# Attention edge stage stores its packed sums as columns, and the output product moves to the node stage

## The chip, the cores and the metric

One core of a Trainium2 chip runs the whole network as one program. The metric is the device time of one execution in microseconds (us), the median of several runs. Besides, one execution was recorded by the hardware profiler; all rows shown here are from that one.

## The reference

Four graph layers follow each other over 50000 nodes and 50000 edges, which are sorted by destination. All numbers are 32-bit floats and D is 128. The change touches the second layer, whose attention is:

```python
K = (x @ Wk.T + bk).reshape(N, HEADS, HEAD_DIM)
V = (x @ Wv.T + bv).reshape(N, HEADS, HEAD_DIM)
Q = x.reshape(N, HEADS, HEAD_DIM)
scores = jnp.sum(K[src] * Q[dst], axis=-1) / np.sqrt(HEAD_DIM)
m = jax.ops.segment_max(scores, dst, num_segments=N)
e = jnp.exp(scores - m[dst])
denom = jax.ops.segment_sum(e, dst, num_segments=N)
attn = e / (denom[dst] + 1e-16)
out = jax.ops.segment_sum(V[src] * attn[:, :, None], dst, num_segments=N)
return out.reshape(N, DIM_H) @ Wo.T + bo
...
h = _batchnorm(x + h_attn, bn1_g, bn1_b)
```

The other layers and the feed-forward part are not touched.

## The kernel before

The program is a row of stages, each with its own block: one in-order instruction stream per engine, semaphores between the streams, and a barrier at the end. A step handles 512 rows (TILES = 4 tiles of P = 128), and S = 98 steps cover all. Two stages matter.

**The attention edge stage** (`attention_edges`, tiles named `e_`) is written as a software pipeline of STEPS = S + 36 loop turns n. In turn n each engine does the pieces of several steps, in the order of the source. TensorE (PE) does: `e_s`, the scores of step n-4 (L1459); `e_hs`, transposes of the gathered source rows of step n (L1467); `e_k` of n-2 (L1474); `e_hd`, transposes of the destination rows of n (L1480); `e_r`, the output product with `wo` of n-33 (L1488); `e_v` of n-29 (L1496); and `e_p`, the packing of n-31 (L1506). Packing sums the weighted messages of a run of equal destinations: a matmul with the 0/1 matrix `pick`, whose column c is 1 where an edge belongs to the c-th run. A step is packed in two halves of HALF = 256 columns; the last column of each holds the sum of the run that goes on in the next half. So many edges can't have more runs than edges, so the first 128 edges of a half fill none of the columns 128 to 254. VectorE (DVE) does in turn n: `e_kq` (L1302), the scan `e_hdt` (L1310), `e_pv` (L1320, messages times weights), `carry_step` of n-32 (L1288, L1290: the open run is added to column 0 in PSUM), then a piece of the softmax of a whole group of GROUP = 14 steps in 11 of every 14 turns, and last `pick` (L1343, L1346). ScalarE (ACT) copies PSUM tiles out (`e_hst`, `e_packed` from `e_r`, `e_att` from `e_p` with the bias `bv`) and issues four loads or stores a turn. GpSimd (POOL) issues four gathers a step (L659), at most four steps ahead of `e_hs`. SyncE (SP) stores each packed half at the row where its first run begins. The halves overlap, so each store waits until the one before it has landed (semaphore `placed`):

```python
for h in range(HALVES):
    if w or h:
        sp.wait_ge(placed, (w * HALVES + h) * 16)
    sp.dma_start(run_rows(scratch["att_runs"], begins[h], HALVES),
                 at(packed, w)[:, HALVES * h:HALVES * h + HALVES, :]).then_inc(placed, 16)
```

Gathers and `e_hs`, `e_k`, `e_hd` end with turn 97; `e_v` begins with turn 29 and `e_p` with turn 31. Turns 31 to 97 are called the full turns below, those from 98 on the closing turns. ps_p, the PSUM tile of `e_p`, is one bank, so `e_p` of a step waits for `e_att` of the step before.

**The attention node stage** (`attention_nodes`, tiles named `n_`): for each 512 nodes SP loads two tiles of runs and the old features `n_h`, ACT loads the other two tiles of runs (its own queue), PE transposes `n_h` and spreads the runs to their nodes with a second 0/1 matrix (`n_t`, L1646), ACT adds the bias `bo` (`n_own`), DVE adds both (`n_tt`, L1619) and ACT stores it. ACT's stream in loop turn i is: load the start rows from SBUF into registers, issue the loads of runs of step i, then `n_own` of step i-3, then the store of step i-5. There are four buffers of runs.

Of the kernel before, what the change touches and what calls it, by code (L numbers as in the profile page):

```python
# [16 lines left out]
P = 128  # L17
# [1027 lines left out]
def attention_edges(nc, size, a, scratch, k):  # L1045
# [10 lines left out]
    with Phase(nc, "e1") as ph:  # L1056
# [13 lines left out]
        att, att_ready = ph.made("att", [D, ROWS])  # L1070
        packed, packed_ready = ph.made("packed", [P, TILES, D], 6)
# [4 lines left out]
        v_done, pack_done, out_done, carry_done = (ph.sem(n) for n in ("v_done", "pack_done", "out_done", "carry_done"))  # L1076
# [31 lines left out]
        ps_hs, ps_hd, ps_k, ps_v, ps_p, ps_r = (ph.ps(n) for n in ("hs", "hd", "k", "v", "p", "r"))  # L1108
# [18 lines left out]
        STEPS = S + 36  # L1127

        @block.sync
        def _(sp):  # L1130
# [23 lines left out]
        def _(dve):  # L1154
# [122 lines left out]
            def carry_step(j):  # L1277

                g, t = divmod(j, GROUP)
                dve.wait_ge(pack_done, j + 1)  # L1280
                if t == 0 and g:
# [3 lines left out]
                for h in range(HALVES):  # L1285
                    own = flat(ps_p)[:, h * HALF:(h + 1) * HALF]
                    new = carry[(j * HALVES + h) % 3]
                    dve.scalar_tensor_tensor(new[:, :], held[0][:, :], half[:, j, HALVES + h:HALVES + h + 1],  # L1288
                                             own[:, HALF - 1:HALF], ALU.mult, ALU.add)
                    done(dve.scalar_tensor_tensor(own[:, 0:1], held[0][:, :], half[:, j, h:h + 1], own[:, 0:1],  # L1290
                                                  ALU.mult, ALU.add))
                    held[0] = new
                dve.sem_inc(carry_done, 1)

            for n in range(STEPS):
# [44 lines left out]
                if 0 <= j < S:  # L1340
                    dve.wait_ge(at(row_in, j), moved(j, j))
                    for t in range(TILES):
                        dve.tensor_scalar(at(pick, j)[:, t, 0:HALF - 1], k.place_row[:, 0:HALF - 1],  # L1343
                                          at(row, j)[:, RUN_SLOT * TILES + t:RUN_SLOT * TILES + t + 1].bitcast(F32), None,
                                          ALU.is_equal)
                    dve.tensor_copy(at(pick, j)[:, :, HALF - 1], values(at(row, j), TAIL)).then_inc(pick_ready, 1)  # L1346

        @block.scalar
        def _(act):
# [12 lines left out]
            for n in range(STEPS):  # L1362
# [66 lines left out]
        def _(pe):  # L1429
# [22 lines left out]
            for n in range(STEPS):  # L1452
# [46 lines left out]
                if 0 <= j < S:  # L1499
                    pe.wait_ge(pv_ready, j + 1)  # L1500
                    pe.wait_ge(pick_ready, j + 1)
                    if j:
                        pe.wait_ge(att_ready, j)
                    for t in range(TILES):
                        h = t // HALVES
                        ins = pe.matmul(flat(ps_p)[:, h * HALF:(h + 1) * HALF], at(pv, j)[:, t, :], at(pick, j)[:, t, :],  # L1506
                                        start=(t % HALVES == 0), stop=(t % HALVES == HALVES - 1))
# [1207 lines left out]
```

## Time and profile before

| | us |
|---|---|
| median of 3 runs (lowest, highest) | 6114.3 (6105.96, 6123.12) |
| the profiled execution: its own time | 6110.7 |
| its span, first to last instruction | 6108.8 |
| edge stage of the attention, first gather to the last store's issue | 1470.2 to 2293.0 |
| node stage of the attention, first issue to last | 2297.3 to 2564.5 |

A stage's time is not visible in the shares of the whole page, since ten other stages are mixed in. The two stages together take about 1100 us of the span and have to be read by windows and by the timeline. "busy" of matmuls is modelled and overlaps, so PE's true pitch is read from the distance of starts. A matmul of 32-bit floats appears as two instructions (x8 for four of them); transposes as one.

### The profile page before, as it was taken

To read this page: it belongs to the slowest core of one execution; us is meant where nothing else is said; L and a number is where in the kernel's file an instruction comes from. 1 tells how busy PE (TensorE), PEld (TensorE's weight loads), DVE (VectorE), ACT (ScalarE), POOL (GpSimd) and SP (SyncE) were. 2 spreads that over 40 slices of the span, in tenths; PEclk is the share of its full clock that TensorE was granted. 3 is DMA by queue.
4 is the path that set the end of the run, shared out by engine and by line. 5 is a ranking of instruction groups with operands and counts; after the bars stand their busy time and mean duration, and the time that the engine had idled before them with its cause. 6 is when DMAs were issued, how large, how long until landed. Compare 5 with 4: busy or idle time off the path is not lost. (4 is left out here: it accounts for less than half of the span.)

```text
span 6108.8 us, 80252 instructions
## 1 busy us (share of the span) xinstructions
PE 3926.9 (64%) x16966; PEld 2588.9 (42%) x16966; DVE 3885.2 (64%) x12531; ACT 1981.9 (32%) x4351; POOL 3027.9 (50%) x2764
## 2 busy tenths in 40 slices
PE   2777733332699985599544457888564877777840
PEld 1555522221377774444333356766321333333310
DVE  4666657773488866667444456666596766766656
ACT  1545422331122222255444432222264222222210
POOL 3566436666666500000455558888402566666630
PEclk7888955555799999999766779899897888888875
DMA  8666656664566528877555557777695011111149
GB/s 268 131 140 140 133 148 191 184 182 143 149 173 176 162 58 266 270 229 226 188 181 171 172 155 130 132 132 131 166 373 196 22 30 33 35 36 37 38 146 375
DMA packets 930549, 954.27 MB, mean 156 GB/s; under 512 B 166711, under 2 KB 617031, under 8 KB 930111
## 3 DMA queue, kind: packets, MB, share of 16 engines
q1 hardware_dynamic: 539178, 545.18, 31.1%
q10 hardware_dynamic: 259157, 259.51, 12.6%
q0 software_dynamic: 131904, 146.31, 12.1%
q8 instruction: 89, 1.46, 0.1%
q14 instruction: 221, 1.81, 0.1%
HBM read 544.69 MB, written 440.07 MB: 161 GB/s over the span
## 5 line engine op out<-in xcount | busy, mean ns | idle before, releaser
L667 POOL DMA_INDIRECT at_first_table<-n_h,n_first_edge x784 | 803.0, 1024 | 1413.2 <-ACT n_h L277 832.0
L2559 PE MATMUL e_m<-e_by_rel,rel_w 128*128 128x512 f32 x1568 | 756.1, 639 | 0.7 <-issue 0.5
L2473 DVE SCALAR_TENSOR_TENSOR e_by_rel<-e_y,e_part_t 128x512 f32<-128x512 f32 x784 | 477.5, 680 | 310.3 <-DMA sum_table<-n_own 223.9
L659 POOL DMA_INDIRECT e_xs<-x_table,e_idx x392 | 381.1, 972 | 434.4 <-DMA e_idx<-idx_table 299.1
L667 POOL DMA_INDIRECT rel_sum_table<-e_res,scat_placed x392 | 393.9, 1005 | 315.4 <-ACT e_res L2525 197.9
L659 POOL DMA_INDIRECT e_x<-x,e_idx x392 | 405.5, 1034 | 279.3 <-issue 172.0
L659 POOL DMA_INDIRECT e_hs<-h_table,e_idx x392 | 420.0, 1071 | 228.6 <-issue 120.1
L947 PE MATMUL n_m<-n_mean,n_pick 128*128 128x129 f32 x784 | 204.7, 442 | 446.7 <-DVE n_pick L1012 231.8
L2559 PEld LDWEIGHTS e_m<-e_by_rel,rel_w 128*128 128x128 f32 x1568 | 318.6, 209 | 371.2 <-issue 371.1
L277 ACT ACTIVATE n_h<-n_x,n_norm_shift,n_norm_rstd 128x128 f32<-128x128 f32 x784 | 322.7, 482 | 182.7 <-issue 116.4
L947 PEld LDWEIGHTS n_m<-n_mean,n_pick 128*128 128x128 f32 x784 | 175.6, 329 | 475.8 <-DVE n_pick L1012 246.9
L2048 PE MATMUL n_o<-w_center_cat,n_h2t 128*128 128x128 f32 x784 | 165.8, 377 | 318.9 <-ACT n_h2t L2015 266.9
L253 ACT ACTIVATE e_norm_std<-e_norm_moments,eps 128x4 f32<-128x4 f32 x196 | 58.3, 297 | 962.3 <-DVE e_norm_moments L245 509.1
L675 POOL DMA_INDIRECT sum_table<-e_res,e_target x196 | 305.0, 1556 | 94.0 <-issue 59.8
L675 POOL DMA_INDIRECT sum_high_table<-e_res,e_target x196 | 312.3, 1593 | 61.8 <-issue 55.1
L2048 PEld LDWEIGHTS n_o<-w_center_cat,n_h2t 128*128 128x128 f32 x784 | 142.2, 272 | 346.9 <-ACT n_h2t L2015 214.4
L2551 PE MATMUL e_t<-ident,e_part 128*128 128x128 f32 x392 | 79.5, 339 | 215.6 <-ACT e_part_t L2513 111.3
L238 DVE BATCH_NORM_STATS2 e_norm_stats<-e_x 128x6 f32<-128x128 f32 x392 | 85.3, 280 | 202.1 <-DMA e_x<-x,e_idx 182.0
L253 ACT ACTIVATE n_norm_std<-n_norm_moments,eps 128x4 f32<-128x4 f32 x294 | 86.0, 292 | 377.6 <-DVE n_norm_moments L245 257.8
L2303 PE MATMUL e_s<-e_same,e_msg 128*128 128x256 f32 x784 | 205.1, 409 | 0.0
L869 PE MATMUL e_c<-e_res,e_pick 128*128 128x130 f32 x392 | 94.9, 330 | 166.6 <-issue 96.1
L2270 PE MATMUL e_p<-w_node,e_hdt 128*128 128x128 f32 x784 | 116.5, 294 | 132.7 <-DVE e_hdt L2206 132.7
(390 smaller groups left out, 10118.1 us busy)
## 6 DMA issues: line engine op xcount, KB each, us to landing
x_table<-n_x ACTq DMA_DIRECT2D x294, 256.0 KB
n_x<-x_table SPq DMA_DIRECT2D x294, 256.0 KB
mean_runs_table<-e_packed SPq DMA_DIRECT2D x196, 130.0 KB
n_mean<-mean_runs_table SPq DMA_DIRECT2D x392, 65.0 KB
at_first_table<-zero ACTq DMA_DIRECT2D x1, 25088.0 KB
e_edge<-edge128T SPq DMA_DIRECT2D x98, 256.0 KB
e_keep<-col_tab_table SPq DMA_DIRECT2D x196, 128.0 KB
n_x<-x SPq DMA_DIRECT2D x98, 256.0 KB
```

What stands on the lines that cost most here:

```text
L253: act.activation(at(self.std, u)[:, :], at(self.moments, u)[:, :, 1], ACT.Sqrt, bias=k.eps[:, :]).then_inc(self.std_done, 1)
L277: last = act.activation(out[:, t, :], x[:, t, :], func, bias=at(self.shift, u)[:, t:t + 1], scale=at(self.rstd, u)[:, t:t + 1])
L659: pool.indirect_dma_start(out=tile[:, t, :], out_offset=None, in_=table, in_offset=bass.IndirectOffsetOnAxis(ap=idx[:, col + t:col + t + 1 ...
L667: pool.indirect_dma_start(out=table, out_offset=bass.IndirectOffsetOnAxis(ap=idx[:, t:t + 1], axis=0), in_=tile[:, t, :], in_offset=None, ...
L675: pool.indirect_dma_start(out=table, out_offset=bass.IndirectOffsetOnAxis(ap=idx[:, t:t + 1], axis=0), in_=tile[:, t, :], in_offset=None, ...
L869: pe.matmul(ps_c[b][:, 0, :], at(pick, u - 10)[:, b, 0:P], at(res, u - 10)[:, low, :], start=True, stop=False)
L947: ins = pe.matmul(at(ps_m, u - 1)[t // HALVES][:, t % HALVES, :], at(pick, u - 1)[:, t, :], at(mean, u - 1)[:, t, 0:D + 1], start=True, st ...
L2048: ins = pe.matmul(at(ps_o, u - 3)[:, t, :], at(h2t, u - 3)[:, t, :], k.w_center_cat[:, :], start=True, stop=True)
L2270: ins = pe.matmul(ps_p[:, t, :], at(hdt, u - 1)[:, t, :], k.w_node[:, :], start=True, stop=True)
L2303: ins = pe.matmul(flat(at(ps_s, u))[:, half], at(msg, u)[:, t, :], at(same, u - 2)[:, t, :], start=(t % 2 == 0), stop=(t % 2 == 1))
L2473: ins = dve.scalar_tensor_tensor(at(by_rel, u - 5)[:, r, :], flat(ps_y), float(r), at(part_t, u - 5)[:, :], ALU.is_equal, ALU.mult)
L2559: ins = pe.matmul(flat(at(ps_m, u - 6)), k.rel_w[:, r, :], at(by_rel, u - 6)[:, r, :], start=(r == 0), stop=(r == RELS - 1))
```

## The change

In the edge stage `e_r` and `e_att` go. The packing matmul per half becomes three: 129 columns of the first 128 edges, the same 129 of the other 128 edges added to them, and the last 127 columns of the other 128 edges alone. The open-run column moves from 255 to 0, and the other columns by one. `ps_p` becomes two banks in turn. ACT copies 2 x 255 columns with the bias `bv` to `packed` ([D, 2, 255]), two turns earlier than before, and STEPS is S + 33. SP stores [128 partitions x 255 floats], 1020 bytes a partition, into a table that is now [D, runs], so a half is 128 pieces of 1020 bytes, 202752 bytes apart, beginning at any multiple of 4 bytes; before it was 256 rows of 512 bytes in one stretch. DVE builds `pick` 128 wide for two of the four tiles and 255 wide for the other two. In `carry_step` the wait for the last operation moves to the start of the next step's.

In the node stage a tile of runs is [D, 128 columns], loaded as 128 pieces of 512 bytes from the same table. PE multiplies it with `wo` (`n_w`), ACT copies that to `n_rows`, and PE spreads it two turns later. Buffers of runs come free at `wo_done`. ACT does `n_own` and `n_rows` of step i-1 where it did `n_own` of step i-3.

```diff
@@ attention_edges, SP @@
-                    sp.dma_start(run_rows(scratch["att_runs"], begins[h], HALVES),
-                                 at(packed, w)[:, HALVES * h:HALVES * h + HALVES, :]).then_inc(placed, 16)
+                    sp.dma_start(scratch["att_runs"][:, bass.ds(begins[h], HALF - 1)], at(packed, w)[:, h, :]
+                                 ).then_inc(placed, 16)
@@ carry_step, DVE @@
                 dve.wait_ge(pack_done, j + 1)
+                if j:
+                    dve.wait_ge(carry_done, j)
...
-                dve.sem_inc(carry_done, 1)
+                    if h < HALVES - 1:
+                        done(ins)
+                ins.then_inc(carry_done, 1)
@@ pick, DVE @@
                     for t in range(TILES):
-                        dve.tensor_scalar(at(pick, j)[:, t, 0:HALF - 1], k.place_row[:, 0:HALF - 1],
+                        there = P if t % HALVES == 0 else HALF - 1
+                        dve.tensor_scalar(at(pick, j)[:, t, 1:1 + there], k.place_row[:, 0:there],
@@ ACT @@
-                j = n - 34
-                if 0 <= j < S:
-                    act.wait_ge(out_done, j + 1)
-                    if j >= 6:
-                        act.wait_ge(placed, (j - 5) * HALVES * 16)
-                    act.activation(at(packed, j)[:, :, :], ps_r[:, :, :], ACT.Copy).then_inc(packed_ready, 1)
                 j = n - 32
                 if 0 <= j < S:
                     act.wait_ge(carry_done, j + 1)
-                    if j >= 2:
-                        act.wait_ge(out_done, j - 1)
-                    act.activation(at(att, j)[:, :], flat(ps_p), ACT.Identity, bias=k.bv[:, :]).then_inc(att_ready, 1)
+                    if j >= 6:
+                        act.wait_ge(placed, (j - 5) * HALVES * 16)
+                    act.activation(at(packed, j)[:, :, :], at(ps_p, j)[:, :, 1:HALF], ACT.Identity, bias=k.bv[:, :]
+                                   ).then_inc(packed_ready, 1)
@@ PE @@
-                j = n - 33
-                if 0 <= j < S:
-                    pe.wait_ge(att_ready, j + 1)
-                    if j:
-                        pe.wait_ge(packed_ready, j)
-                    for t in range(TILES):
-                        ins = pe.matmul(ps_r[:, t, :], at(att, j)[:, t * P:(t + 1) * P], k.wo[:, :], start=True, stop=True)
-                    ins.then_inc(out_done, 1)
...
-                    if j:
-                        pe.wait_ge(att_ready, j)
+                    if j >= 2:
+                        pe.wait_ge(packed_ready, j - 1)
@@ attention_nodes, PE @@
+                    if begun(i - 3):
+                        pe.wait_ge(rows_ready, i - 2)
                     for t in range(TILES):
+                        ins = pe.matmul(at(ps_w, u)[:, t, :], at(runs, u)[:, t, :], k.wo[:, :], start=True, stop=True)
+                    ins.then_inc(wo_done, 1)
+                j = i - 2
+                if live(j, S):
+                    pe.wait_ge(pick_ready, j + 1)
+                    pe.wait_ge(rows_ready, j + 1)
@@ attention_nodes, ACT @@
                     if begun(i - 4):
-                        act.wait_ge(spread_done, i - 3)
+                        act.wait_ge(wo_done, i - 3)
...
-                j = i - 3
+                j = i - 1
                 if live(j, S):
                     act.wait_ge(turned, j + 1)
...
+                    act.wait_ge(wo_done, j + 1)
+                    if begun(j - 3):
+                        act.wait_ge(spread_done, j - 2)
+                    act.activation(at(rows, u - 1)[:, :, :], at(ps_w, u - 1)[:, :, :], ACT.Copy).then_inc(rows_ready, 1)
```

PE's stream of one full turn of the edge stage, before:

```order
L1459 MATMUL e_s<-e_kq,e_head_win 112x512
L1467 MATMUL e_hs<-ident,e_hs 128x128 x4
L1474 MATMUL e_k<-e_hst,wk 128x512
L1480 MATMUL e_hd<-ident,e_hd 128x128 x4
L1488 MATMUL e_r<-wo,e_att 128x128 x4
L1496 MATMUL e_v<-wv,e_hst 128x128 x4
L1506 MATMUL e_p<-e_pick,e_pv 128x256 x4
```

And of the changed kernel, the same turn:

```order
L1459 MATMUL e_s<-e_kq,e_head_win 112x512
L1467 MATMUL e_hs<-ident,e_hs 128x128 x4
L1474 MATMUL e_k<-e_hst,wk 128x512
L1480 MATMUL e_hd<-ident,e_hd 128x128 x4
L1488 MATMUL e_v<-wv,e_hst 128x128 x4
L1498 MATMUL e_p<-e_pick,e_pv 128x129
L1499 MATMUL e_p<-e_pick,e_pv 128x129
L1501 MATMUL e_p<-e_pick,e_pv 128x127
L1498 MATMUL e_p<-e_pick,e_pv 128x129
L1499 MATMUL e_p<-e_pick,e_pv 128x129
L1501 MATMUL e_p<-e_pick,e_pv 128x127
```

`e_r` is gone and the 1024 packing columns have become 770.

ACT's stream of one turn of the node stage, before (from the register loads to the store):

```order
L165 TENSOR_LOAD starts
L165 ISA x4
L1659 ISA
L1659 DMA n_runs<-att_runs_table 128x128
L1659 ISA
L1659 DMA n_runs<-att_runs_table 128x128
L1666 ACTIVATE n_own<-n_h,bo 128x512
L1671 DMA tt_table<-n_tt 128x512
```

And of the changed kernel:

```order
L165 TENSOR_LOAD starts
L165 ISA x4
L1664 REGISTER_ALU
L1664 DMA n_runs<-att_runs_table 128x128
L1664 REGISTER_ALU
L1664 DMA n_runs<-att_runs_table 128x128
L1671 ACTIVATE n_own<-n_h,bo 128x512
L1676 ACTIVATE n_rows<-n_w 128x512
L1680 DMA tt_table<-n_tt 128x512
```

One instruction more, and the two ACTIVATEs belong to the step whose runs were issued one turn before, where the one of before belonged to the step of three turns before.

## Rows read from the trace of the kernel before

**Rows 1.** Windows: length, busy PE, PEld, DVE, ACT, POOL, then PEclk, DMA share, GB/s.

```profile
1700.00:2090.00 390.00, 377.80 (x2210) 284.28 (x2209) 334.96 (x867) 110.65 (x192) 259.01 (x230) 1.00 0.63 177
2130.00:2295.00 165.00, 136.69 (x812) 114.19 (x810) 105.97 (x365) 41.61 (x71) 0.00 (x0) 0.96 0.21 56
2310.00:2570.00 260.00, 151.35 (x1136) 134.10 (x1135) 176.38 (x282) 64.78 (x95) 0.00 (x0) 0.97 0.91 285
```

**Rows 2.** Timeline of PE, one full turn: start, length, line, operation, count.

```profile
1905.35 1.11 PE L1459 MATMUL e_s<-e_kq,e_head_win 128*112 128x512 f32 x2
1908.03 1.06 PE L1488 MATMUL e_r<-wo,e_att 128*128 128x128 f32 x8
1908.92 1.06 PE L1496 MATMUL e_v<-wv,e_hst 128*128 128x128 f32 x8
1909.82 1.89 PE L1506 MATMUL e_p<-e_pick,e_pv 128*128 128x256 f32 x8
1911.64 0.20 PE L1444 MATMUL e_x<-ident,e_top 112*1 112x8 f32 x2
```

**Rows 3.** Timeline of DVE in the same turn.

```profile
1909.84 1.13 DVE L1343 TENSOR_SCALAR e_pick<-place_row,e_row 128x255 f32<-128x255 f32 x4
1910.89 0.16 DVE L1346 COPY e_pick<-e_row 128x4 f32<-128x4 f32 x1
```

**Rows 4.** Groups by line, 1700 to 2090 us: count, busy, mean ns, idle before.

```profile
L659 POOL DMA_INDIRECT e_hs<-h_table,e_idx x230 | 261.6, 1137 | 131.3 <-issue 73.1 <-PE e_hs L1467 58.2
L1320 DVE TENSOR_TENSOR e_pv<-e_v,e_weight_t 128x512 f32<-128x512 f32 x57 | 38.5, 675 | 40.0 <-remote 35.1 <-PE e_p L1506 2.7 <-issue 2.2
L1264 DVE RECIPROCAL e_spare<-e_back 112x512 f32<-112x512 f32 x4 | 13.4, 3352 | 0.1
```

**Rows 5.** Waits of SP's queue, 1700 to 2090 us: total, times, longest.

```profile
SPq L1140 <- DMA att_runs_table<-e_packed: 52.6, 26, 3.7
SPq L1139 <- DMA att_runs_table<-e_packed: 28.8, 19, 3.1
```

**Rows 6.** Timeline of ACT and PE, closing turns.

```profile
2232.53 0.69 ACT L1397 ACTIVATE e_att<-e_p,bv 128x512 f32<-128x512 f32 x1 [3.18 <-DVEq L1293]
2233.36 1.96 PE L1506 MATMUL e_p<-e_pick,e_pv 128*128 128x256 f32 x8 [0.28 <-ACT e_att L1397]
2236.89 0.69 ACT L1397 ACTIVATE e_att<-e_p,bv 128x512 f32<-128x512 f32 x1 [3.18 <-DVEq L1293]
```

**Rows 7.** SP's stores at the end of the edge stage, and in all; the last ACT copies.

```profile
2270.69 22.67 SPq L1140 DMA_DIRECT2D att_runs_table<-e_packed  x12
...
L1140 SPq DMA_DIRECT2D att_runs_table<-e_packed x196: 3/372/701, 1695.0 to 2293.0; - x196
L1368 ACT ACTIVATE e_hst<-e_hs x98: 597/597/600, 1477.9 to 2126.8; 128x512 f32<-128x512 f32 x98
```

**Rows 8.** Node stage: SP's issues of runs, duration and first and last start.

```profile
L1595 SPq DMA_DIRECT2D n_runs<-att_runs_table x196: 332/333/2312, 2297.3 to 2564.5; - x196
```

**Rows 9.** Timeline at the start of the node stage, SP and PE.

```profile
2298.28 0.43 SPq L1599 DMA_DIRECT2D n_h<-h_table  x1
2301.24 1.11 PE L1638 MATMUL n_h<-ident,n_h 128*128 128x128 f32 x4 [15.39 <-DMA n_h<-h_table]
```

**Rows 10.** Timeline of ACT and PE inside the node stage.

```profile
2423.10 1.06 PE L1646 MATMUL n_t<-n_pick,n_runs 128*128 128x128 f32 x8
2423.30 0.69 ACT L1666 ACTIVATE n_own<-n_h,bo 128x512 f32<-128x512 f32 x1 [2.16 <-PE n_h L1638]
2423.31 0.36 ACTq L1671 DMA_DIRECT2D tt_table<-n_tt  x1
2424.82 0.86 ACTq L1659 DMA_DIRECT2D n_runs<-att_runs_table  x2
```

**Rows 11.** SP's queue by window: earlier node stage (820 to 1420 us), then this one (2310 to 2570).

```profile
q1 hardware_dynamic: 67802, 49.80, 33.8%
q1 hardware_dynamic: 40301, 36.81, 47.7%
```

More of the change, by code:

```diff
@@ L1107, in attention_edges @@
              "den_back_col", "weight_turned", "factor_spread"))
-        ps_hs, ps_hd, ps_k, ps_v, ps_p, ps_r = (ph.ps(n) for n in ("hs", "hd", "k", "v", "p", "r"))
+        ps_hs, ps_hd, ps_k, ps_v = (ph.ps(n) for n in ("hs", "hd", "k", "v"))
+        ps_p = [ph.ps(f"p{u}", (D, HALVES, HALF)) for u in range(2)]
         ps_s, ps_x = ph.ps("s", (P, ROWS)), ph.ps("x", (P, ROWS))
@@ L1285, in carry_step @@
                 for h in range(HALVES):
-                    own = flat(ps_p)[:, h * HALF:(h + 1) * HALF]
+                    own = at(ps_p, j)[:, h, :]
                     new = carry[(j * HALVES + h) % 3]
                     dve.scalar_tensor_tensor(new[:, :], held[0][:, :], half[:, j, HALVES + h:HALVES + h + 1],
-                                             own[:, HALF - 1:HALF], ALU.mult, ALU.add)
-                    done(dve.scalar_tensor_tensor(own[:, 0:1], held[0][:, :], half[:, j, h:h + 1], own[:, 0:1],
-                                                  ALU.mult, ALU.add))
+                                             own[:, 0:1], ALU.mult, ALU.add)
+                    ins = dve.scalar_tensor_tensor(own[:, 1:2], held[0][:, :], half[:, j, h:h + 1], own[:, 1:2],
+                                                   ALU.mult, ALU.add)
                     held[0] = new
-                dve.sem_inc(carry_done, 1)
+                    if h < HALVES - 1:
+                        done(ins)
+                ins.then_inc(carry_done, 1)
             for n in range(STEPS):
@@ L1342, in _ @@
                     for t in range(TILES):
[L1343 removed]
+                        there = P if t % HALVES == 0 else HALF - 1
+                        dve.tensor_scalar(at(pick, j)[:, t, 1:1 + there], k.place_row[:, 0:there],
                                           at(row, j)[:, RUN_SLOT * TILES + t:RUN_SLOT * TILES + t + 1].bitcast(F32), None,
                                           ALU.is_equal)
[L1346 removed]
+                    dve.tensor_copy(at(pick, j)[:, :, 0], values(at(row, j), TAIL)).then_inc(pick_ready, 1)
         @block.scalar
@@ L1501, in _ @@
                     pe.wait_ge(pick_ready, j + 1)
-                    if j:
-                        pe.wait_ge(att_ready, j)
[L1504 to L1507, printed above, removed]
+                    if j >= 2:
+                        pe.wait_ge(packed_ready, j - 1)
+                    for h in range(HALVES):
+                        low, high, own = HALVES * h, HALVES * h + 1, at(ps_p, j)[:, h, :]
+                        pe.matmul(own[:, 0:P + 1], at(pv, j)[:, low, :], at(pick, j)[:, low, 0:P + 1], start=True, stop=False)
+                        pe.matmul(own[:, 0:P + 1], at(pv, j)[:, high, :], at(pick, j)[:, high, 0:P + 1], start=False,
+                                  stop=True)
+                        ins = pe.matmul(own[:, P + 1:HALF], at(pv, j)[:, high, :], at(pick, j)[:, high, P + 1:HALF],
+                                        start=True, stop=True)
                     ins.then_inc(pack_done, 1)
@@ L1576, in attention_nodes @@
         h1, h1_in = ph.loaded("h1", [P, TILES, D])
-        runs, low_in = ph.loaded("runs", [P, TILES, D])
+        runs, low_in = ph.loaded("runs", [D, TILES, P])
         high_in = ph.dma_sems("high_in")
         pick, pick_ready = ph.made("pick", [P, TILES, P], 4)
-        own, own_ready = ph.made("own", [D, TILES, P])
+        own, own_ready = ph.made("own", [D, TILES, P], 4)
+        rows, rows_ready = ph.made("rows", [P, TILES, D], 3)
         tt, tt_ready = ph.made("tt", [D, TILES, P], 4)
         tt_out = ph.dma_sems("tt_out")
-        turned, spread_done, stats_done = ph.sem("turned"), ph.sem("spread_done"), ph.sem("stats_done")
-        ps_h, ps_t = ph.banks("h"), ph.banks("t")
+        turned, wo_done, spread_done, stats_done = (ph.sem(n) for n in ("turned", "wo_done", "spread_done", "stats_done"))
+        ps_h = ph.banks("h")
+        ps_w, ps_t = ([ph.ps(f"{n}{u}") for u in range(3)] for n in ("w", "t"))
         block = ph.ctx.enter_context(nc.Block())
@@ L1592, in body @@
                     if begun(i - 4):
-                        sp.wait_ge(spread_done, i - 3)
+                        sp.wait_ge(wo_done, i - 3)
                     for t in range(HALVES):
-                        sp.dma_start(at(runs, u)[:, t, :], scratch["att_runs"][bass.ds(begins[t], P), :]
+                        sp.dma_start(at(runs, u)[:, t, :], scratch["att_runs"][:, bass.ds(begins[t], P)]
                                      ).then_inc(at(low_in, u), 16)
@@ L1641, in body @@
                     pe.wait_ge(at(high_in, u), moved(i, u, HALVES))
-                    pe.wait_ge(pick_ready, i + 1)
-                    if begun(i - 2):
-                        pe.wait_ge(tt_ready, i - 1)
+                    if begun(i - 3):
+                        pe.wait_ge(rows_ready, i - 2)
                     for t in range(TILES):
-                        ins = pe.matmul(at(ps_t, u)[:, t, :], at(runs, u)[:, t, :], at(pick, u)[:, t, :], start=True,
-                                        stop=True)
+                        ins = pe.matmul(at(ps_w, u)[:, t, :], at(runs, u)[:, t, :], k.wo[:, :], start=True, stop=True)
[5 more added lines that the diff above has]
+                    if begun(j - 3):
+                        pe.wait_ge(tt_ready, j - 2)
+                    for t in range(TILES):
+                        ins = pe.matmul(at(ps_t, u - 2)[:, t, :], at(rows, u - 2)[:, t, :], at(pick, u - 2)[:, t, :],
+                                        start=True, stop=True)
                     ins.then_inc(spread_done, 1)
-            each_step(body, S, 0)
+            each_step(body, S, 2)
         @block.scalar
```

18 lines of the change are left out of this document (9 added, 9 removed).

## The prediction

> **What bounds the kernel now.** The change lives in two stages, so I read windows first. In the full turns of the edge stage PE is busy 378 of 390 us at full clock, DVE 335, POOL 259, and the DMA engines are busy 63% of the time; in the node stage it is the other way round, DMA 91% and PE 151 of 260 us [rows 1]. The reader is to see that the edge stage is short of engine time and the node stage of transfers, and that the change moves work from the first to the second.
>
> Next the timeline of one full turn. PE starts `e_s` at 1905.35 and has finished `e_p` at 1911.64, 6.29 us without a gap [rows 2]. 57 `e_pv` in 390 us are 6.84 us a turn [rows 1, 4], so a turn is somewhat longer than PE's own work. The rest is DVE: in 11 of 14 turns it has a piece of the group's softmax to do, and one of these holds a reciprocal of 3.35 us and several scans [rows 4]; such turns are DVE's. DVE's only wait of size is the 40.0 us before `e_pv` [rows 4], which comes after the previous turn's `e_p`, the last thing that PE does in a turn. So the full turns alternate: a turn costs what the slower of PE and DVE needs in it, and DVE's idle time (0.70 us a turn, 40.0 over 57) is what a faster PE can give at most.
>
> In the closing turns the pitch of `e_att` is 4.36 us [rows 6] and PE and DVE go round in a ring: `e_p` waits for `e_att`, `e_att` for `carry_step`, that for `e_p`. But right beside it is SP: twelve stores in 22.67 us, the last issue taking 0.37, make 2.03 us from store to store, 4.06 a turn [rows 7]. The last store is issued at 2293.0, the last `e_hst` at 2126.8 [rows 7]: 166 us of closing.
>
> In the node stage SP issues 196 loads of runs in 267.2 us, 2.76 us a step [rows 8]. ACT there waits 2.16 us for `n_h` before it does `n_own` [rows 10], and that costs nothing, because it works three steps behind its own loads.
>
> **Full turns.** Removed from PE: eight instructions of `e_r`, 1908.03 to 1908.92, 0.89 us. `e_p` takes 1.82 us for eight instructions, of which the last part is the change to `e_x`; 1024 columns become 770, and twice as many columns per instruction as in `e_v` took twice as long, so I take 1.82 x 770/1024 = 1.37, a saving of 0.45 [rows 2]. PE's turn falls from 6.29 to 4.95. If six weight loads per step instead of four were to limit it, the saving on `e_p` would be nothing; that is the other bound, and still leaves 5.4, under DVE's mean.
>
> DVE: four `pick` pieces take 1.05 us, 0.26 each [rows 3]. Two become half as wide: 0 to 0.26 saved, I take 0.15 as part of a short instruction is fixed. The last handshake of `carry_step` goes off its path, about 0.1. ACT loses one copy and is busy 28% of the window [rows 1]: nothing. DVE's mean turn without waits was 6.84 - 0.70 = 6.14; less 0.25 it is 5.9. In the three turns of 14 without softmax, and in a few with a short piece, DVE needs about 4.15 and PE 4.95, so roughly 0.2 a turn of waiting remains: 6.1. I add 0.05 for the other two chains, which come near. POOL is busy 261.6 us and stands 73.1 us between instructions for nothing that is shown, 5.9 us a turn [rows 4]; it waits 58.2 us for `e_hs`, which is the slack it has. SP waits 81.4 us for stores to land in this window [rows 5], so under the load of the other transfers a store takes more than the 2.03 us of the end. So 6.15 instead of 6.84: 0.69 x 67 turns (31 to 97) = **-46 us**. Bounds: 5.9 gives -63, 6.45 (POOL or SP as the bound) gives -26.
>
> **Closing turns.** The ring opens: `e_p` has two banks, `e_att` and `e_r` are gone. PE's work falls to `e_v` and `e_p`, 0.89 + 1.37, DVE's to about 2.3 outside the softmax pieces. What comes next is SP with its serial stores. Each is 128 pieces of 1020 bytes in place of 256 of 512; no row shows such a piece, and I bound it by the row of now, 2.03 us, plus or minus 0.2. From the last `e_hst` on 31 to 32 steps are to be stored, 4.06 to 4.2 each, about 130, and the turn with the reciprocal, once at the start, holds SP up by some 9: 139 instead of 166, **-27 us**. Bounds: -38 with quicker stores, -14 with slower.
>
> **Node stage.** SP's and the other queues' bytes are the same. PE gets `n_w`, priced as `n_t`, 8 instructions of 0.11 at full clock, 0.89 us: 2.2 us of PE in a step of 2.76, covered. ACT gets a copy of 0.59 us. The price is in the order. Before, ACT had three steps between its loads of runs and the first wait that stands behind them. Now, in turn i, it issues runs i and then waits for `wo_done` of step i-1, whose runs it issued one turn before; runs i+1 stay queued behind that wait. So two turns can't be shorter than one trip round: from the first to the second issue 0.45, landing L, `n_w` 0.9 and a semaphore 0.1, the issue of `tt` and after it the register loads until the next runs, which were 1.51 us from 2423.31 to 2424.82 [rows 10]; in sum 3.0 + L. What is L? At the stage's start, with little in flight, `n_h` was issued at 2298.28 and used by PE at 2301.24: 2.96 us [rows 9]. Inside the stage the queue on the engines is longer, DMA share 0.91 [rows 1]. A store of 128 KB landed and was followed up in 2.03 [rows 7], the low end. I take L = 3.5, since a longer step lowers the load but the run loads now stand behind `tt` in the same queue: (3.0 + 3.5)/2 = 3.25 us a step, +0.49 x 98 = **+48 us**. Bounds: L of 2.5 gives 2.75, no cost at all; L of 4.5 gives 3.75, +97.
>
> **Against the rules.** The Trainium skill, "DMA: Bandwidth & Descriptors", section Anatomy of one DMA, gives a fixed cost of about 2.0 us and a variable one of bytes over 436 GB/s. By it a 64 KB load lands after 2.15 us (an estimate of that page), the round trip would be (3.0 + 2.15)/2 = 2.6, below 2.76, and the stage would not lengthen. The row says 2.96 for 256 KB at light load, 0.4 more than the page's 2.6 for that size, and so L of the loaded stage lies above it too.
>
 In the earlier node stage SP's queue loads rows of 520 bytes, which begin anywhere: 33.8% of 16 engines over 600 us for 49.80 MB are 65 us per MB, against 47.7% over 260 us for 36.81 MB, 54 us per MB, with aligned rows [rows 11]. The sizes are mixed differently, so the rows allow such a cost and don't prove it.
>
> **Rivals.**
> 1. The node stage hides its new wait (runs land within 2.5 to 2.9 us when the load eases). For it: the 2.96 of [rows 9] is of a transfer four times as large. Against: DMA share 0.91. Then +0 to +19, net about -60: 6055. Chance 0.2.
> 2. Node stage decides, slower than before: the wait on `wo_done` with L at 4.3 or more. That is the point where (3.0 + L)/2 = 3.65, +87, outweighs what a somewhat weaker edge stage gives (-65). For it: ACT already waits 2.2 us for a transpose that itself waits for a load [rows 10]; and if pieces at odd places take half as long again, the runs' third of the bytes lengthens the queue. At L = 4.8 the stage costs +112 and the net is +39: 6153. Chance 0.18.
> 3. The full turns don't follow PE. POOL's 5.9 and SP's serial stores under load become the bound at 6.5. For it: [rows 4, 5]. Against: both have slack of four and six steps. Then -23 - 27 + 48 = about 0: 6113. Chance 0.17.
> 4. The forecast, -46 - 27 + 48 = -25. Chance 0.45.
>
> **Numbers.** The profiled execution took 6110.7; less 25 is 6086. It stands 3.6 below the median of the runs, so 6089 in terms of that. The forecast's own range is 6065 to 6112. With the rivals' share on both sides, 6045 to 6145. A difference under 0.3%, 18 us, can't be told from no change. The forecast lies for the larger part beyond it (0.28 of 0.45), rival 1 wholly, rival 3 hardly (0.03), rival 2 never: faster 0.51. Same: 0.17 of the forecast, 0.13 of rival 3, 0.02 of rival 2: 0.32. Slower: 0.17.
>
> **What the changed profile would show.** Full turns: start-to-start of PE's `e_s` at 6.1 on average, PE's work in it 5 us, the wait before `e_pv` down from 40 us to under 15 in 57 turns, DVE busy over 90%. Closing turns: SP's stores one after the other at 2.0 us with ACT's `e_packed` waiting for them. Node stage: SP's 196 loads of runs over about 315 us in place of 267, ACT's queue waiting for `n_w` before `n_rows`, PE waiting for ACT's runs and no longer for `n_h`, and a DMA share near 0.78. The prediction is wrong if the node stage keeps its 2.76 us a step, if stores of 1020-byte pieces take clearly other than 2.03 us, or if the full turns stay above 6.4.

## The result, and the profile after

The changed kernel took 6145.6 us (median of 6 runs, 6137.22 to 6158.71), the kernel before 6115.11 beside it: ratio 1.0054, interval 1.0041 to 1.0068, so slower by half a per cent. The forecast was 6089, in a range of 6045 to 6145. In a second set of runs the ratio was 1.0078 (1.0050 to 1.0107). In a third set, on a chip that had run the kernel before in 6103 us earlier, the kernel before took 5629.73 us and the ratio was 0.9994 (0.9984 to 1.0005). One and the same program runs at two levels, 9% apart, and the change is worth something else at each; this turned out to be the core of the case. I call these the slower and the faster level; all runs that were made together, one after the other on one chip, lay at the same one.

Where the time went in the profiled executions at the slower level, before and after in us:

| | before | after | difference | forecast |
|---|---|---|---|---|
| start of the edge stage to its 33rd `e_hst` | 1477.9 to 1686.8 | 1473.9 to 1681.0 | -2 | 0 |
| full turns, 33rd to 98th `e_hst` | 440.0 | 441.6 | +2 | -46 |
| closing, last `e_hst` to the last store | 166.2 | 146.3 | -20 | -27 |
| node stage, first runs to the last store of `tt` | 274.1 | 332.8 | +59 | +48 |

The rest, -4 ahead of the stage and +6 behind it, lies in stages that the change doesn't touch.

The windows of the changed kernel, as in [rows 1], and the groups by line of DVE and POOL, 1700 to 2090 us, as in [rows 4]:

```profile
1700.00:2090.00 390.00, 323.68 (x1946) 236.71 (x1947) 317.15 (x849) 81.10 (x132) 238.06 (x226) 0.96 0.61 174
2126.00:2272.00 146.00, 90.00 (x665) 80.42 (x664) 98.36 (x364) 24.76 (x38) 0.00 (x0) 0.90 0.20 62
2285.00:2590.00 305.00, 229.85 (x1826) 214.39 (x1826) 170.62 (x272) 111.99 (x182) 0.00 (x0) 0.97 0.81 236
```

```profile
L1314 DVE TENSOR_TENSOR_SCAN e_hdt<-e_keep,e_hdt,e_hd 128x512 f32<-128x512 bf16 x56 | 71.0, 1267 | 12.9 <-remote 12.9
L1324 DVE TENSOR_TENSOR e_pv<-e_v,e_weight_t 128x512 f32<-128x512 f32 x57 | 38.6, 676 | 47.9 <-remote 39.1 <-PE e_p L1501 6.2 <-issue 2.5
```

```profile
L659 POOL DMA_INDIRECT e_hs<-h_table,e_idx x226 | 238.9, 1057 | 152.1 <-PE e_hs L1467 60.0 <-issue 60.0 <-remote 32.2
```

The reader is to see that PE did lose the work (378 of 390 us busy before, 324 now) and that no engine took its place: PE 83%, DVE 81%, POOL 61%, transfers 61%. DVE waits more than before, 47.9 us before `e_pv` and 12.9 before `e_hdt` where it had 40.0 and nothing, and 52 us of that have a "remote" releaser. A piece of the timeline shows what stands behind this word (DVE, POOL and PE; start, length, line):

```profile
1702.75 0.39 PE L1501 MATMUL e_p<-e_pick,e_pv 128*128 128x127 f32 x2
1704.30 0.60 PE L1467 MATMUL e_hs<-ident,e_hs 128*128 128x128 f32 x4
1705.45 0.94 POOL L659 DMA_INDIRECT e_hs<-h_table,e_idx  x1 [0.30 <-issue]
1705.59 0.60 PE L1480 MATMUL e_hd<-ident,e_hd 128*128 128x128 f32 x4
1707.79 0.69 DVE L1324 TENSOR_TENSOR e_pv<-e_v,e_weight_t 128x512 f32<-128x512 f32 x1 [2.96 <-remote]
1708.58 0.94 POOL L659 DMA_INDIRECT e_hs<-h_table,e_idx  x1 [2.18 <-remote]
1708.63 1.13 PE L1488 MATMUL e_v<-wv,e_hst 128*128 128x128 f32 x8 [2.43 <-DVE e_pv L1324]
```

PE's `e_p` is recorded as ended at 1703.14, but the trace's record of its semaphore stands at 1707.66, and those of `e_s`, `e_hs`, `e_k` and `e_hd` behind it at 1707.75 to 1707.91, all at once. (The profile writes "remote" where the semaphore that ended a wait has no instruction that ended shortly before.) DVE waits for the first of them, POOL for `e_hs`, PE then for DVE: from 1706.40 to 1707.79 none of the three works. I call this a late release. To count them over the turns from the 34th to the 98th `e_hst`, each of PE's products is matched with the first record of its semaphore behind its recorded end and ahead of the next turn's; records are missing, so not all can be matched. 119 of 355 came over 1 us late in the changed kernel, 43 of 386 in the kernel before.

### The profile page after: what moved, and what is told of

Same layout as the page of the kernel before. It is cut to its first block and busy times, and to the rows that moved or that the text cites. A ratio compares the mean times of both kernels' runs of the same rounds, so it can differ in the third digit from the quotient of the medians.

```text
span 6149.7 us, 80931 instructions
## 1 busy us (share of the span) xinstructions
PE 3900.5 (63%) x17358; PEld 2589.7 (42%) x17358; DVE 3866.4 (63%) x12531; ACT 1986.0 (32%) x4351; POOL 3014.4 (49%) x2764
## 5 line engine op out<-in xcount | busy, mean ns | idle before, releaser
L667 POOL DMA_INDIRECT at_first_table<-n_h,n_first_edge x784 | 802.7, 1024 | 1457.7 <-ACT n_h L277 870.5
L659 POOL DMA_INDIRECT e_hs<-h_table,e_idx x392 | 402.2, 1026 | 246.6 <-issue 104.1
L2568 PEld LDWEIGHTS e_m<-e_by_rel,rel_w 128*128 128x128 f32 x1568 | 317.9, 209 | 370.0 <-issue 370.0
```

The source lines that it names most:

```text
L659: pool.indirect_dma_start(out=tile[:, t, :], out_offset=None, in_=table, in_offset=bass.IndirectOffsetOnAxis(ap=idx[:, col + t:col + t + 1 ...
L667: pool.indirect_dma_start(out=table, out_offset=bass.IndirectOffsetOnAxis(ap=idx[:, t:t + 1], axis=0), in_=tile[:, t, :], in_offset=None, ...
L2568: ins = pe.matmul(flat(at(ps_m, u - 6)), k.rel_w[:, r, :], at(by_rel, u - 6)[:, r, :], start=(r == 0), stop=(r == RELS - 1))
```

## The experiments

The measure for the full turns is the distance from the 33rd to the 98th `e_hst`, divided by 65. All edits are made to the changed kernel, if nothing else is said.

| us a full turn | slower level | faster level |
|---|---|---|
| kernel before | 6.77, 6.85 | 6.60 |
| changed kernel | 6.79, 6.74 | 5.98 |
| with the node stage's longer lag | 6.75, 6.86 | 5.93 |
| and a later start of the gathers (behind `e_v`; behind `e_p`) | 6.97; - | 5.92; 5.92 |
| `e_v` done twice | 7.00 | - |
| zero stores moved out | 6.73 | - |
| one gather of four | - | 6.03, 6.05 |
| no gathers | 6.00 | - |
| kernel before, no gathers | - | 6.63, 6.64, 6.63 |

**Is PE what sets the full turn?** (e_v2)

```diff
-                    for t in range(TILES):
+                    for t in range(2 * TILES):
+                        t = t % TILES
                         ins = pe.matmul(ps_v[:, t, :], at(hst, j)[:, t * P:(t + 1) * P], k.wv[:, :], start=True, stop=True)
```

> The changed kernel, with the four products e_v of each turn of the edge stage done twice (1.06 us more of PE's work a turn, the same result). If PE's work sets the full turn, as the forecast had it, 6.79 us a turn becomes 7.6 to 7.9 us. If PE has slack that the change opened (1.34 us less work a turn for no gain), it stays within 6.75 to 7.0 us. The closing turns (4.0 us bound by SP's stores, PE at 60%) should stay at 146 us by both.

Measured: 7.00 us a turn, at the top of the second range; 1.06 us more work cost 0.21. PE has the slack: most of the added work is hidden. The whole took 6160.69 us in one run; closing was 153 us, 7 more than expected.

**Gathers out** (e_plain; the same for the kernel before in e_before_plain, q_before_plain and z_before_plain)

```diff
-                gather(pool, at(hs, i), scratch["h1"], idx[:, i, :], 0, at(hs_in, i))
...
                 act.dma_start(at(hd, i)[:, :, :], in_order(scratch["at_first"], i)).then_inc(at(hd_in, i), 16)
+                act.dma_start(at(hs, i)[:, :, :], in_order(scratch["h1"], i)).then_inc(at(hs_in, i), 16)
```

> The changed kernel; in the edge stage the source rows are not gathered by POOL's four indirect transfers a turn but loaded by one plain transfer of 512 rows in order, issued by ACT behind e_hd's (so other rows are attended: the gather is left out, the bytes stay). Full turns are counted on e_hst from its 33rd to its 98th instruction: 6.79 us in the changed kernel, 6.77 before. Theory POOL: PE's finished products are handed over late while POOL issues its gathers (the releases come about 1.1 us behind the fourth gather's end), and these holds make DVE's waits of 49 us in the 380 us looked at; without gathers the turn falls to 6.2 us or less. Theory transfers: the 16 DMA engines' load or the landings set the turn; the bytes are the same, so it stays at 6.7 or more. Theory DVE: DVE's own work with its start-up gaps is 6.1 a turn and ACT's order the rest; 6.6 to 6.8.

Measured: 6.00 us, 5993.63 in all. DVE's waits in the full turns, total, times, longest, and the window itself:

```profile
DVE e_pv L1323 <- PE e_p L1501: 12.4, 16, 0.8
DVE e_kq L1305 <- PE e_k L1474: 7.8, 11, 1.9
```

```profile
1600.00:1960.00 360.00, 328.72 (x2055) 243.50 (x2054) 333.00 (x897) 86.25 (x141) 0.00 (x0) 0.97 0.65 199
```

No remote releaser is left, and with the same bytes, or nearly, the transfers' share is even a little higher. DVE is busy 92%, as forecast for the changed kernel. Counted as above, none of 437 semaphores of PE came over 1 us late. So the turn that the forecast wanted (6.15) exists, and the gathers stand between it and the kernel at this level. What the edit takes out is both POOL's issuing and the scattered transfers themselves.

> The kernel before, with the same replacement as in the changed kernel without gathers: the edge stage's source rows come by one plain transfer of 512 rows in order, issued by ACT (the gather is left out, other rows are attended). If the gathers' holds hid the change's gain, the full turns of this kernel stay above the 6.00 us of the changed one, since here PE has its 6.29 us of work a turn: 6.4 to 6.6 us, and the change is then worth 0.4 to 0.6 us a turn where POOL issues nothing. If PE's work never mattered, both stand at 6.0 to 6.1 us.

This run fell on the faster level (the kernel before took 5607.38 us beside it): 6.63 us, 5538.38 in all. Two more runs, meant for the slower level, fell on the faster one too: 6.64 and 6.63.

> The kernel before without gathers in the edge stage (a plain transfer in their place), once more: the first run of it fell on a chip that runs the kernel before in 5607 us. On a chip of 6110 us, where the changed kernel without gathers had full turns of 6.00 us: theory POOL expects 6.5 to 6.7 us here (PE's pace, no holds), so that the change is worth 0.5 to 0.7 us a turn once nothing is gathered, as the forecast had it. If the chip and not the gathers set both, 6.0 to 6.1.

> The kernel before without the edge stage's gathers, for the one cell that is missing. Where the kernel before takes 6110 us: if the late releases come only with POOL's gathers, its full turns stand at 6.6 us, as they do (twice, 6.63) where the kernel before takes 5620 us, against 6.00 us of the changed kernel without gathers; 6.75 to 6.85 us if something else holds them. Where it takes 5620 us: 6.63 a third time.

So the kernel before stands at 6.63 us where nothing is gathered, with PE as its pace, and the cell at the slower level stays empty.

**Less load from transfers** (e_nozero)

```diff
-                if n < S:
-                    act.dma_start(rows_of(scratch["rel_sum"], n), k.zero[:, :]).then_inc(zeroed, 16)
+            for n in range(S):
+                act.dma_start(rows_of(scratch["rel_sum"], n), k.zero[:, :]).then_inc(zeroed, 16)
```

> The changed kernel, with the 98 stores of zeros to rel_sum taken out of the edge stage's turns and issued by ACT in a row behind its loop (same bytes, other place). That takes one of ACT's four transfer issues, 0.46 us, and 256 KB out of each turn. Theory transfers: the full turn falls by 0.3 us or more from 6.79. Theory POOL (holds while the gathers are issued): it stays within 0.1 us. Theory ACT's order (e_hst waits behind e_packed and the issues): it falls by some 0.2 us. The end of the stage becomes longer by the stores' own time, 50 to 90 us, so the total tells nothing.

Measured: 6.73 us, within 0.1 of 6.79, with the window's DMA share at 0.51 in place of 0.61 (1700 to 2080 us), and DVE still waits 47 us there for remote releasers. Neither this load nor ACT's order explains the missing 0.6 us a turn. (6166.25 us in all.)

**The node stage's order** (e_node; again as r_node and z_node). The first piece is PE's `n_t`, the second ACT's `n_own` and `n_rows`; their buffer indices go along.

```diff
                     ins.then_inc(wo_done, 1)
-                j = i - 2
+                j = i - 3
...
-                j = i - 1
+                j = i - 2
                 if live(j, S):
                     act.wait_ge(turned, j + 1)
```

> The changed kernel, with one more turn between the output product and its reader in the node stage: ACT's n_own and n_rows go from step i-1 to step i-2, PE's spread product n_tt from i-2 to i-3. Nothing else. In-order theory: the wait on wo_done of the step just loaded stands before the next loads, and that costs 3.28 us a step against 2.76 in the kernel before; with two steps in hand the loads of n_runs go back to 2.8 us a step or less, the stage gives back 45 to 55 us, and the kernel takes 6092 to 6102 us, 0.2 to 0.4% under the kernel before. Rival, column loads themselves are slow (512 B pieces of 128 partitions, a third product and copy): the pitch stays at 3.1 us or more and the kernel stays over 6125 us.

Measured: 6113.71 us, ratio 1.0012 (0.9988 to 1.0037). SP's issues of runs, to be read beside [rows 8]; first the changed kernel, then this one:

```profile
L1592 SPq DMA_DIRECT2D n_runs<-att_runs_table x196: 332/333/1592, 2273.1 to 2591.0; - x196
```

```profile
L1592 SPq DMA_DIRECT2D n_runs<-att_runs_table x196: 332/333/1165, 2273.2 to 2554.3; - x196
```

Over 97 steps that is 3.28 against 2.90 us. The longer lag gives back 34 us from the first runs to the last store of `tt` (332.8 to 298.8; 27 us of the whole in a later set that had both kernels, 6157.8 and 6130.77), less than the 45 to 55 expected, and the whole stayed over the 6092 to 6102; 0.15 us a step above the kernel before stay. The order is shown as the larger part of the price, not as all of it.

**Does it matter when the gathers start?** (e_late_v and r_late_v, on top of the longer lag; e_late_pack waits for `pack_done` at i - 34 instead)

```diff
                     pool.wait_ge(hs_turned, i - 3)
+                if i >= 33:
+                    pool.wait_ge(v_done, i - 32)
```

> The changed kernel with the node stage's longer lag, and in the edge stage POOL starts the gathers of turn i+4 only when PE has ended e_p of turn i's step (before: when e_hs was turned, half a turn earlier). All four gathers stay. Theory POOL: the holds then fall on e_s, e_hs, e_k, e_hd of the next turn, which DVE wants some 4 us later, and no longer on e_p and e_v: 6.3 to 6.6 us a full turn against 6.79 (6.75 in the kernel with the longer lag). If the start makes no difference, since POOL's four gathers fill 4.7 of the turn wherever they begin: 6.7 to 6.9 us.

> As the one above, but POOL starts when PE has ended e_v (about 1.4 us earlier in PE's turn). The hold then falls on e_p, whose carry DVE does some 2.8 us later: 6.4 to 6.7 us a full turn if the place counts, and more than with the start behind e_p; 6.7 to 6.9 us if it doesn't.

Measured: 5.92 us both, 5568.15 and 5565.76 in all. It looked like a success, but beside them the kernel before took 5607.38 us, not 6110, and not one semaphore of PE's was late (none of 431 and 436). The next set was to separate the two:

> The kernel before, unchanged, for its trace beside the others of this call on the same chip: one chip ran it in 6103 us (median of 13), another in 5607 us. Where the chip is one that runs it in about 5600 us, theory holds expects: no wait of DVE's e_pv put down to a remote releaser (35 us in the 380 us looked at, in the first trace), early turns of 5.2 us instead of 6.5 (as in the two late-start kernels), and full turns that still stand at 6.6 to 6.8 us, PE's own pace (6.63 in this kernel without gathers). Where it is one of about 6110 us: 6.77 as in the first trace.

> The changed kernel, unchanged. On a chip of 5600 us theory holds expects what the forecast had: full turns of 5.9 to 6.1 us (PE and DVE free to follow, -0.6 to -0.7 a turn, some -45 us), closing turns -20 us, node stage +50 to +55 us, in sum -10 to -20 us against the kernel before. If the holds aren't what separates the chips, the full turns stand within 0.1 us of the kernel before and the changed kernel is 30 us slower there too. On a chip of 6110 us: +0.5%, as measured.

> The changed kernel with the longer lag in the node stage (n_own, n_rows at i-2, spread at i-3). Node stage 2.9 to 3.0 us a step against 3.2 to 3.3, so 20 to 35 us less than the changed kernel on any chip; against the kernel before -35 to -50 us on a chip of 5600 us, within 0.3% on one of 6110 us.

> The kernel with the longer lag and POOL's gathers started only when PE has ended e_v, beside the same without the later start on the same chip. It ran at 5.92 us a full turn on the chip of 5600 us. If the later start did that, the kernel above stands at 6.3 us or more there; if the chip did it, the kernel above stands within 0.1 us of this. On a chip of 6110 us the start counts only if the full turn falls from 6.75 to under 6.6 us.

It fell on the slower level. Kernel before 6.85 us a full turn (6107.4 in all); changed kernel 6.74, ratio 1.0078; longer lag 6.86, ratio 1.0029 (1.0013 to 1.0045), node stage 2.91 us a step; later start 6.97, ratio 1.0036 (1.0015 to 1.0057). The later start gives nothing (0.11 us a turn more, no more than the two traces of the kernel with the longer lag differ from each other); the 5.92 was the level's. My idea that the place of the gathers in PE's turn counts is refuted for the start behind `e_v`; the start behind `e_p` was not run at this level.

**Both kernels at the faster level** (q_before, q_after, q_g1)

> The kernel before, unchanged, for its trace on this call's chip. Full turns of 6.6 to 6.85 us on any chip: PE's own pace lies at 6.6, the holds add little since PE is behind them all the same. Early turns, which wait for landings, 5.2 us on a chip of 5600 us and 6.4 on one of 6110.

> The changed kernel, unchanged. On a chip of 5600 us: full turns of 5.9 to 6.1 us, so that the change gains 40 to 50 us there, against 50 lost in the node stage and 20 gained behind the last turn: 0.2 to 0.4% faster than before. On a chip of 6110 us: full turns of 6.7 to 6.85 us and 0.5 to 0.8% slower, as twice measured.

Measured: 6.60 and 5.98 us a full turn, ratio 0.9994 (0.9984 to 1.0005). DVE's waits in the full turns, first the kernel before, 1600 to 1960 us, then the changed one, 1600 to 1930, and the windows of the latter (full turns, node stage):

```profile
DVE e_pv L1320 <- PE e_p L1506: 25.8, 23, 1.9
DVE e_pv L1320 <- issue: 0.9, 1, 0.9
```

```profile
DVE e_pv L1324 <- PE e_p L1501: 11.7, 16, 0.8
DVE e_kq L1306 <- PE e_k L1474: 6.2, 10, 1.6
```

```profile
1600.00:1930.00 330.00, 301.73 (x1887) 224.74 (x1887) 305.90 (x824) 79.30 (x129) 229.57 (x218) 0.96 0.72 197
2110.00:2390.00 280.00, 211.95 (x1683) 197.01 (x1682) 158.16 (x252) 103.39 (x169) 0.00 (x0) 0.97 0.82 239
```

No remote releaser in either, with all four gathers on POOL; late semaphores 0 of 494 and 0 of 434. DVE is busy 93%. The differences by part: full turns -40, closing -23 (169.7 to 147.0), node stage +56 (273.4 to 329.8), in sum -6 of 5630, while the median moved by -2. So here the forecast's step for the full turns holds, and the node stage eats it; the gain of 0.2 to 0.4% that I expected did not come.

DVE's work in a full turn is the same at both levels: 5.5 us, from its busy share in the windows above and 6.79 and 5.98 us a turn. Its idle time is 1.27 us at the slower and 0.44 at the faster, and this is the whole of the 0.81 between the two.

> The changed kernel with one gather of four left on POOL. On a chip of 6110 us (none: 6.00, four: 6.74 to 6.79): theory POOL expects 6.0 to 6.2 us a full turn and under 5 us of waits of DVE with a remote releaser in 380 us (27 to 39 us with four gathers). A turn above 6.4 us would say that one gather costs as much as four.

6.05 us, the same as with the first run of it:

> The changed kernel, with one of the four gathers of a turn kept on POOL and the other three tiles loaded by one plain transfer of ACT's (three quarters of the gather are left out; the bytes stay). Theory POOL: a hold lasts from the product to about 1.1 us behind POOL's last gather, so with one gather of 0.94 us in place of four in 4.7 us the holds have under 2.1 us to cover, most of it hidden: 6.0 to 6.2 us a full turn (four gathers 6.79, none 6.00). If it were the gathers' transfers, and not POOL's issuing, a quarter of them would leave a quarter of the 0.79 us, the same 6.2; a turn over 6.4 us would speak against both, for a price of the first gather.

6.03. Both ran at the faster level, where four gathers cost no more (5.98), so they say nothing on how the late releases depend on the number of gathers.

**The version that keeps both gains** (z_node)

> The changed kernel with the longer lag in the node stage, once more, against the kernel before on this call's chip. Where the kernel before takes about 5620 us: full turns of 5.98 us as in the changed kernel there (6.60 in the kernel before), node stage 2.9 to 3.0 us a step (3.25 without the lag, 2.75 before), so 40 us from the full turns and 20 from the closing ones stand against 20 in the node stage: 5575 to 5600 us, 0.5 to 0.8% faster than before. Where it takes about 6110 us: the full turns give nothing, and it stands at +0.0 to +0.4%, as twice measured.

5567.6 us against 5596.85, ratio 0.9932 (0.9911 to 0.9954), inside the expected gain and 7 us under the expected time, since the kernel before was faster here too. Full turns 5.93 us, node stage 2.97 us a step:

```profile
L1592 SPq DMA_DIRECT2D n_runs<-att_runs_table x196: 332/333/1141, 2050.2 to 2338.6; - x196
```

```profile
2080.00:2330.00 250.00, 203.18 (x1644) 190.68 (x1642) 154.02 (x247) 95.98 (x162) 0.00 (x0) 0.97 0.88 260
```

The transfers' share is back at 0.88, near the 0.91 of [rows 1]. This kernel beats both others at the faster level; at the slower it stands at +0.1 and +0.3%.

## Why the prediction was wrong

**Full turns: the step that failed.** "DVE's idle time (0.70 us a turn, 40.0 over 57) is what a faster PE can give at most", and then that PE's fall from 6.29 to 4.95 gives nearly all of it. Of the 40.0 us, [rows 4] put 35.1 to "remote" and only 2.7 to PE's `e_p`. I read them all as PE's length. At the level of that trace late releases are part of it, and they don't shorten with PE's work: in the kernel before PE is so long (6.6 us) that they hide behind it for the larger part (6.77 to 6.85 against 6.60 without them, 0.2 a turn). In the changed kernel nothing hides them, more of them count (119 against 43), and the turn is 0.8 us longer with them (6.79 against 5.98), more than the 0.6 that the edit saves where there are none. -46 was forecast (the 6.84 us a turn that it starts from, 390 over 57, is 6.77 by the distance of starts, so the same working would have given -42), +2 measured; at the faster level it was -40, with the working of the forecast intact: DVE at 93%, waits before `e_pv` of 12 us. Nor was the reading of the 40.0 us wholly false: at the faster level the same wait is still 25.8 us in 360, all of it put to `e_p`, 0.47 us a turn of the 0.70. What it left out is that late releases would take the place of PE's length once that was gone.

**Rival 3** named this outcome with another mechanism, POOL or SP as the bound. Neither is: POOL is busy 61% and stands 60 us waiting for `e_hs`, and at the faster level POOL and SP issue all the same transfers at 5.98 us a turn. Its price for the full turns (-23) was also too favourable against the +2 measured.

**Closing turns: right.** -20 at the slower level, -23 at the faster, forecast -27, bounds -38 and -14. SP's stores run back to back at the end, as said: 33 issues in one row of the timeline,

```profile
2201.41 67.84 SPq L1140 DMA_DIRECT2D att_runs_table<-e_packed  x33
```

2.11 us from store to store (67.84 less the last issue's 0.33, over 32) where 2.03 was taken, and over 64 stores that is 5 of the 7 us that are missing. A store of 1020-byte pieces costs about what one of 512-byte pieces did.

**Node stage: right in its mechanism, 11 us short.** Two turns as one trip of ACT's, seen in ACT and PE of the changed kernel:

```profile
2440.17 0.83 ACTq L1664 DMA_DIRECT2D n_runs<-att_runs_table  x2
2443.01 0.85 ACTq L1664 DMA_DIRECT2D n_runs<-att_runs_table  x2
2443.79 1.13 PE L1642 MATMUL n_w<-wo,n_runs 128*128 128x128 f32 x8 [1.02 <-issue]
2444.96 0.60 ACT L1676 ACTIVATE n_rows<-n_w 128x512 f32<-128x512 f32 x1 [0.31 <-PE n_w L1642]
2446.49 0.34 ACTq L1664 DMA_DIRECT2D n_runs<-att_runs_table  x1
```

Runs issued at 2440.17 are multiplied at 2443.79, copied at 2444.96, and only then the loads at 2446.49 go out: 6.32 us for two steps. SP's 196 loads took 317.9 us (315 forecast), which by the formula is L = 3.55 (3.5 taken). Read from the timeline of steps 10 to 89 instead, the time from ACT's second issue to `n_w` is 3.4 us on average. The wait binds in most turns, not in all: `n_rows` starts right behind `n_w` in 51 of these 80 steps, and in the others ACT itself came later. The rest of the +59 stands behind the last load: the longer tail of `tt` stores, which the sum left out. Rival 1 (hidden) is refuted, rival 2's L of 4.3 wasn't reached; that the kernel is slower is due to the missing 46 above all: of the miss of some 65 us in the span it is 48, this stage 11 and the closing turns 7. By the Trainium skill's fixed cost of about 2.0 us ("DMA: Bandwidth & Descriptors", Anatomy of one DMA) the stage would have kept its 2.76. That section fits transfers that GpSimd issues, while these are issued by SP and ACT; the 3.4 us measured lie well above the 2.15 that it gives. The Trainium skill's rule on odd starting addresses ("DMA: Bandwidth & Descriptors", How a descriptor splits into AXI transactions) shows no large effect: in the packets of the trace a 512-byte piece of the node stage takes 27 ns in the median in both kernels, 30 ns on average before and 32 after.

**What stays open.** That the gain is there where no release is late is shown twice: by the changed kernel at the faster level, and at the slower one by e_plain, where the late releases go with the gathers. It isn't known what the late releases are. The large ones of `e_p` came mostly 1.0 to 1.8 us behind the end of POOL's fourth gather (16 of the 17 over 3 us) and along with its landings (1706.40 and 1707.66 above), which speaks for a common cause, but is only seen side by side. Whether POOL's issuing or the gathers' transfers do it wasn't separated, since the kernels made for it fell on the faster level; POOL's instruction for a gather takes the same at both (median 944 and 947 ns), so it isn't this that becomes slower. And what puts a whole set of runs on one level or the other was not found: chips 1 and 3 were each seen at both.

## What to carry to other kernels

Before an idle time is booked as what a faster engine can give, look at who the profile says ended it: 35.1 of 40.0 us "remote" were a sign that something besides PE's length might end them, though not of how much. A wait that hides behind a long engine comes out when the engine is made shorter. And in an in-order stream, a new consumer goes more than one turn behind its own loads where the buffers allow it: two turns in place of one gave back 27 to 40 us of the node stage in three comparisons of traces, for no work at all.

## What the runs showed of the hardware

The kernel before took 6097 to 6130 us in one set of runs and 5592 to 5619 in another on the same chip. The TensorE clock doesn't explain it: over the span it was granted at 0.812 and 0.844 of full speed, but at 1.00 in the full turns of the kernel before at both levels. What differs in the traces is the semaphores: with the gathers in place 11 to 36% of PE's came over 1 us late at the slower level and none at the faster, and of the 64 landings of a step's four gathers about 20 to 28 are on record at the slower level, nearly all at the faster. Turns that wait for gathers (the first 32 of the stage) take 6.3 to 6.6 us there and 5.2 to 5.3 here; without gathers they take 3.8 us there and 3.7 to 3.8 here.

The slower level slows down only stretches in which GpSimd issues indirect transfers, and not all of these. Two traces of the kernel before, one from each level, are 6108.8 and 5622.6 us long. Followed along SyncE's transfers, which are the same in both, the whole difference arises in stretches with indirect transfers (487 us); the 1334 us without any take 1 us less at the slower level than at the faster. The node stage, which has none, is the same at both, to be read beside [rows 8]:

```profile
L1595 SPq DMA_DIRECT2D n_runs<-att_runs_table x196: 332/333/1218, 2145.8 to 2412.2; - x196
```

So the two levels part where GpSimd's gathers and scatters run, and why they do so there is open.
